# Rounding feed-forward weights to eight bits: absolute value on ScalarE, maximum on VectorE, additions on GpSimd, blocks in pairs

## The reference

```python
def _l2_normalize_complex(z):
    return z / jnp.sqrt(jnp.sum(jnp.abs(z) ** 2, axis=-1, keepdims=True))
def _quantized_matmul(x, w, scale):
    wq = w.astype(jnp.float8_e4m3fn).astype(x.dtype)
    return jnp.einsum('bsi,io->bso', x, wq) * scale

# x: (4, 512, 512) f32; W_q, W_kv, W_o: (512, 512); gate_w, up_w: (512, 1536); down_w: (1536, 512)
n = layernorm(x)
q, kv = (n @ W_q.T), (n @ W_kv.T)            # as (4, 512, 16 heads, 32)
qf  = _l2_normalize_complex(jnp.fft.fft(q, axis=-1))
kvf = jnp.cumsum(_l2_normalize_complex(jnp.fft.fft(kv, axis=-1)), axis=1)
x = x + jnp.fft.ifft(qf * kvf, axis=-1).real.reshape(4, 512, 512) @ W_o.T
n = layernorm(x)
fuse = silu(_quantized_matmul(n, gate_w, gate_scale)) * _quantized_matmul(n, up_w, up_scale)
out = x + _quantized_matmul(fuse, down_w, down_scale)
```

## Time and profile before

| | |
|---|---|
| median of three runs | 485.88 us |
| the profiled execution: time, span | 485.9 us, 483.9 us |
| TensorE busy | 439.1 us (91%) |
| VectorE busy | 315.1 us (65%) |
| ScalarE busy | 169.1 us (35%) |
| GpSimd busy | 174.2 us (36%) |
| loads and stores | 26.14 MB, mean 54 GB/s |

### The profile page before, as it was taken

One profiled execution on the slowest core, in us unless ns is written; L12 is line 12 of the kernel. 1 busy time (PEld: TensorE's weight loads), 2 busy tenths in 40 slices (PEclk: granted clock), 3 DMA queues, 4 the chain that ended last, 5 costly groups with the idle time before them and its releaser, 6 DMA issues.

```text
span 483.9 us, 5568 instructions
## 1 busy us (share of the span) xinstructions
PE 439.1 (91%) x1976; PEld 283.8 (59%) x1976; DVE 315.1 (65%) x542; ACT 169.1 (35%) x280; POOL 174.2 (36%) x161
## 2 busy tenths in 40 slices
PE   5997888997667979999998999999999999999995
PEld 4783465674333636667754666677655676555554
DVE  5999797999999966733585456443685536432234
ACT  3724433433321314533352335224533334222230
POOL 0485565686565875103006541040044400300002
PEclk9997998999898979999999999999999999999999
DMA  8933021323112300006000010013000000110002
GB/s 249 365 90 128 0 67 43 89 87 108 45 44 88 88 23 22 1 1 218 0 2 0 9 36 0 1 63 113 1 0 2 0 1 0 44 45 1 0 0 87
DMA packets 14811, 26.14 MB, mean 54 GB/s; under 512 B 2112, under 2 KB 2368, under 8 KB 14784
## 3 DMA queue, kind: packets, MB, share of 16 engines
q1 hardware_dynamic: 14496, 25.77, 16.5%
q10 hardware_dynamic: 288, 0.02, 0.0%
HBM read 21.57 MB, written 4.19 MB: 53 GB/s over the span
## 4 chain that ended last, share of the span: by engine, by line
PE 59%; DVE 6%; POOL 3%; issue 2%; ACT 1%; DVEq 0%; POOLq 0%
PE bg L383 14%; PE bd L399 14%; PE bu L383 14%; PE ba L307 9%; PE ba L341 6%; DVE qk L780 2%; PE ba L320 1%; PE ba L350 1%; POOL qk L1056 1%; POOL qk L1045 1%; POOL ks L1047 1%; DVE mq L705 1%; DVE hT L716 1%; PE ba L329 1%; DVE tu L797 1%
## 5 line engine op out<-in xcount | busy, mean ns | idle before, releaser
L399 PE MATMUL bd<-dw,fu 128*128 128x512 f32 x376 | 99.9, 408 | 3.9 <-DVE fu L852 3.9
L383 PE MATMUL bu<-hT,gu 128*128 128x512 f16 x384 | 93.0, 386 | 7.4 <-DVE ff L847 7.4
L383 PE MATMUL bg<-hT,gu 128*128 128x512 f16 x384 | 92.8, 385 | 0.5 <-ACT sl L569 0.5
L399 PEld LDWEIGHTS bd<-dw,fu 128*128 128x128 f32 x376 | 70.0, 190 | 20.0 <-DVE fu L852 4.9
L847 DVE SCALAR_TENSOR_TENSOR ff<-bu,us,sl 128x512 f32<-128x512 f32 x48 | 35.9, 748 | 66.1 <-PE bu L383 64.3
L383 PEld LDWEIGHTS bu<-hT,gu 128*128 128x128 f16 x384 | 38.0, 100 | 55.2 <-DVE ff L847 8.9
L307 PE MATMUL ba<-wf,xTs 128*128 128x512 f32 x288 | 69.1, 395 | 1.1 <-DVE wf L696 1.1
L1065 POOL TENSOR_TENSOR h<-ff,h 128x512 f32<-128x512 f32 x14 | 17.5, 1281 | 128.3 <-DVE ff L869 128.3
L383 PEld LDWEIGHTS bg<-hT,gu 128*128 128x128 f16 x384 | 35.3, 99 | 47.8 <-issue 11.3
L307 PEld LDWEIGHTS ba<-wf,xTs 128*128 128x128 f32 x288 | 54.0, 188 | 13.2 <-DVE wf L696 1.3
L569 ACT ACTIVATE sl<-bg,gs 128x512 f32<-128x512 f32 x48 | 33.0, 687 | 64.3 <-PE bg L383 63.5
(11 more groups left out here) (159 smaller groups left out, 529.8 us busy)
## 6 DMA issues: line engine op xcount, KB each, us to landing
h<-x_dram SPq DMA_DIRECT2D x16, 256.0 KB, 4.0
out_dram<-h SPq DMA_DIRECT2D x16, 256.0 KB, 2.0
hT<-gate_w_dram SPq DMA_DIRECT2D x12, 256.0 KB, 2.7
xTr<-xT_dram SPq DMA_DIRECT2D x12, 256.0 KB, 3.3
hT<-up_w_dram SPq DMA_DIRECT2D x12, 256.0 KB, 2.6
hT<-down_w_dram SPq DMA_DIRECT2D x12, 256.0 KB, 2.6
hT<-w_q_dram SPq DMA_DIRECT2D x4, 256.0 KB, 4.0
gu<-w_kv_dram SPq DMA_DIRECT2D x4, 256.0 KB, 5.7
```

Source lines behind the costliest of these rows:

```text
L383: m = e.matmul(bk[:, :], gu[:, c, 4 * w + k, col:col + P], hT[:, b % 2, part, k, :], start=k == 0 and part == 0, stop=k == KT - 1 and part ...
L399: m = e.matmul(bd[t][:, :], fu_at(n)[:, part, P * t:P * t + P], dw[:, i, :], start=i == 0 and part == 0, stop=i == NI - 1 and part == 1)
```

## The change

- The blocks are taken in pairs: 18 pairs of 128x1024, each loaded by one DMA, each step one instruction over the pair.
- `m` is now found in two steps. ScalarE takes the absolute value times 2^20, rounded to bf16 (`act_size`), and VectorE takes the maximum with a constant, in place (`dve_unit`). For gate and up `m` lies in the place of the rounded weights, for down in `mq`.
- The additions are on GpSimd for 16 pairs (`pool_round`) and on VectorE for pairs 10 and 11 (`dve_round`).
- The first eight pairs go around four pair places, that is eight blocks: the old four and the four of `h` for batch 1, which hold xT of batch 0 before and x of batch 1 after. Later pairs use the two old pair places.
- `ROUNDING`, its table of steps and the places go. Steps are written out ahead of the loop; in it, `SIZES` and `ROUNDS` say for each iteration of batch 0 which pairs are done at its end. SyncE issues the loads of all pairs ahead of the other loads and stores of the loop.
- `E` and `Q` are used again for results of the head norms in place of `ya` and `yy`.

ScalarE has `act_size` 0 and 1 behind the copies of the folds of q and of k, 2 behind the first two projections, 3 behind the next two, 4 behind the first two `act_ks`, 5 behind the last two, 6 ahead of the third `act_pT`, 7 behind the first projection pair of batch 1. In the loop it stands at the end of the iteration, ahead of `act_x`.

```diff
+NPR = 18
+NEAR = 8
+SIZES = {0: (8, 9), 1: (9, 11), 2: (11, 12), 3: (12, 13), 4: (13, 14), 5: (14, 15), 6: (15, 16), 7: (16, 17), 8: (17, 18)}
+ROUNDS = {0: (7, 9), 1: (9, 10), 3: (12, 13), 4: (13, 14), 5: (14, 15), 6: (15, 16), 7: (16, 17), 8: (17, 18)}
 def tenancies():
...
-        mq = sb("mq", [P, 3, 512], BF16)
+        mq = sb("mq", [P, 2, 2, 512], BF16)
...
+        pairs = []
         for c in range(3):
             for w, src in ((0, gate_w), (1, up_w)):
-                for k in range(KT):
-                    chunks.append((src[P * k:P * k + P, 512 * c:512 * c + 512], gu[:, c, 4 * w + k, :], c, None))
-            for i in range(4 * c, 4 * c + 4):
-                chunks.append((down_w[P * i:P * i + P, :], dw[:, i, :], c, i))
-        NC_ = len(chunks)
-        steps, rounded_on = rounding_table(NC_)
+                for k in (0, 2):
+                    pairs.append((src[P * k:P * k + 2 * P, 512 * c:512 * c + 512],
+                                  gu[:, c, 4 * w + k:4 * w + k + 2, :]))
+            for i in (4 * c, 4 * c + 2):
+                pairs.append((down_w[P * i:P * i + 2 * P, :], dw[:, i:i + 2, :]))
+        assert len(pairs) == NPR
         AT, BEFORE, LEAVES = tenancies()
+        def stage_at(n):
+            slot = 2 * (n % 4 if n < NEAR else n % 2)
+            return stage[:, slot:slot + 2, :] if slot < 4 else h[:, 1, slot - 4:slot - 2, :]
+        def stage_before(n):
+            if n < NEAR:
+                return (n - 4 if n > 3 else None), n // 4 + 1
+            return (n - 4 if n < NEAR + 2 else n - 2), (NEAR // 4 + (n - NEAR) // 2 + 1)
+        def size_at(n):
+            return mq[:, n % 2, :, :] if n % 6 > 3 else pairs[n][1].bitcast(BF16)
         def rounded(n):
-            what, count = rounded_on[n]
-            return (p_rd if what == "p" else v_rd), count
-        def rounded_all(ns):
-            on = {}
-            for n in ns:
-                what, count = rounded_on[n]
-                on[what] = max(on.get(what, 0), count)
-            return [(p_rd if what == "p" else v_rd, count) for what, count in on.items()]
+            if n in (10, 11):
+                return v_rd, n - 9
+            return p_rd, (n + 1 if n < 10 else n - 1)
+        def stage_landed(n):
+            return d_st[n % 4 if n < NEAR else n % 2], 16 * stage_before(n)[1]
...
+        def act_size(e, n):
+            e.wait_ge(*stage_landed(n))
+            if n == 6:
+                e.wait_ge(s_fold, 8)
+            if n == 12:
+                e.wait_ge(s_wohi, KT)
+            if n % 6 > 3 and n > 5:
+                e.wait_ge(*rounded(n - 6))
+            e.activation(size_at(n), stage_at(n), ACT.Abs, scale=2.0 ** 20).then_inc(a_size, 1)
...
-        def dve_expo(e, n):
-            m = mq[:, n % 3, :]
-            top = stage[:, n % 4, :].bitcast(U16).rearrange("p (n t) -> p n t", t=2)[:, :, 1]
-            e.wait_ge(d_st[n % 4], 16 * (n // 4 + 1))
-            if n >= 3:
-                e.wait_ge(*rounded(n - 3))
-            e.tensor_scalar(m.bitcast(U16), top, 0x7F80, 0x0040, ALU.bitwise_and, ALU.bitwise_or).then_inc(v_ex, 1)
-            e.wait_ge(v_ex, 2 * n + 1)
-            e.tensor_scalar(m, m, 1.5 * 2.0 ** -6, 2.0 ** 20, ALU.max, ALU.mult).then_inc(v_ex, 1)
-        def round_chunk(e, n):
-            what, count = rounded_on[n]
-            _, dst, c, i = chunks[n]
-            added, done = (p_add, p_rd) if what == "p" else (v_add, v_rd)
-            piece, m = stage[:, n % 4, :], mq[:, n % 3, :]
-            e.wait_ge(v_ex, 2 * n + 2)
-            e.tensor_tensor(piece, piece, m, ALU.add).then_inc(added, 1)
-            e.wait_ge(added, count)
-            if i is None and c == 2 and n % 12 == 0:
-                e.wait_ge(s_wohi, KT)
-            if i is None and c == 1 and n % 12 == 0:
-                e.wait_ge(s_fold, 8)
-            e.tensor_tensor(dst, piece, m, ALU.subtract).then_inc(done, 1)
-        def dve_spare(e, place):
-            for what, n in steps.get(place, ()):
-                if what == "e":
-                    dve_expo(e, n)
-                elif what == "d":
-                    round_chunk(e, n)
+        def dve_unit(e, n):
+            e.wait_ge(a_size, n + 1)
+            e.tensor_scalar(size_at(n), size_at(n), 1.5 * 2.0 ** 14, None, ALU.max).then_inc(v_unit, 1)
+        def dve_round(e, n):
+            e.wait_ge(v_unit, n + 1)
+            e.tensor_tensor(stage_at(n), stage_at(n), size_at(n), ALU.add).then_inc(v_add, 1)
+            e.wait_ge(v_add, rounded(n)[1])
+            e.tensor_tensor(pairs[n][1], stage_at(n), size_at(n), ALU.subtract).then_inc(v_rd, 1)
...
+                    if b == 0 and i in SIZES:
+                        for pair in range(*SIZES[i]):
+                            dve_unit(e, pair)
+                        if i in (2, 3):
+                            dve_round(e, 8 + i)
...
+        def pool_round(e, first, end):
+            for n in range(first, end):
+                e.wait_ge(v_unit, n + 1)
+                e.tensor_tensor(stage_at(n), stage_at(n), size_at(n), ALU.add).then_inc(p_add, 1)
+                e.wait_ge(p_add, rounded(n)[1])
+                e.tensor_tensor(pairs[n][1], stage_at(n), size_at(n), ALU.subtract).then_inc(p_rd, 1)
...
         def gpsimd_program(e):
             pool_x(e, 0, 0)
             pool_x(e, 0, 1)
-            for place in ("a0", "a1", "a2", "a3", "a4"):
-                pool_spare(e, place)
+            pool_round(e, 0, 4)
             pool_ks(e, 0, 0)
             pool_ks(e, 0, 1)
-            pool_spare(e, "a5")
+            pool_round(e, 4, 5)
             pool_product(e, 0, 0)
-            pool_spare(e, "p0")
             pool_ks(e, 0, 2)
             pool_ks(e, 0, 3)
             pool_product(e, 0, 1)
+            pool_round(e, 5, 6)
             pool_product(e, 0, 2)
-            pool_spare(e, "p1")
             pool_product(e, 0, 3)
-            pool_spare(e, "p2")
-            pool_spare(e, "p3")
-            pool_x(e, 1, 0)
-            pool_x(e, 1, 1)
-            pool_spare(e, "p4")
-            pool_x(e, 1, 2)
-            pool_x(e, 1, 3)
-            for place in ("p5", "p6", "p7", "p8", "p9", "p10", "p11", "p12"):
-                pool_spare(e, place)
+            for k in range(KT):
+                pool_x(e, 1, k)
+            pool_round(e, 6, 7)
...
                         if i == 4:
                             pool_product(e, nxt, 0)
-                    if b == 0:
-                        pool_spare(e, f"split{i}")
-                        if i == 1:
-                            pool_spare(e, "stats")
-                    if nxt < NB and 5 <= i <= 7:
-                        pool_product(e, nxt, i - 4)
-                    if b == 0:
-                        pool_spare(e, f"end{i}")
+                        if 5 <= i <= 7:
+                            pool_product(e, nxt, i - 4)
+                    if b == 0 and i in ROUNDS:
+                        pool_round(e, *ROUNDS[i])
...
+        def sp_weights(e, first, end):
+            for n in range(first, end):
+                before, _ = stage_before(n)
+                if before is not None:
+                    e.wait_ge(*rounded(before))
+                elif n >= 2:
+                    for k in (2 * n - 4, 2 * n - 3):
+                        e.wait_ge(a_x, k + 1)
+                        e.wait_ge(*x_low_done(0, k))
+                e.dma_start(stage_at(n), pairs[n][0].rearrange("(k p) n -> p k n", p=P)).then_inc(stage_landed(n)[0], 16)
...
-            for place in ("a0", "a1", "a2", "a3", "a4", "a5", "p0"):
-                sp_spare(e, place)
-            sp_x(e, 1)
-            for place in ("p1", "p2", "p3", "p4"):
-                sp_spare(e, place)
+            sp_weights(e, 4, 8)
             sp_xT(e, 1, 2)
             sp_xT(e, 1, 3)
-            for place in ("p5", "p6", "p7", "p8", "p9", "p10", "p11", "p12"):
-                sp_spare(e, place)
+            sp_weights(e, 8, 10)
+            sp_x(e, 1)
+            sp_weights(e, 10, NPR)
```

More of the change, by code:

```diff
@@ L45, in constants @@
             np.concatenate([inv, tri, ones], 1).astype(np.float32))
-ROUNDING = {
[5 rows of a table removed]
[L54 to L70, removed]
-            if what == "e":
[L72 to L80, removed]
+NPR = 18
+NEAR = 8
+SIZES = {0: (8, 9), 1: (9, 11), 2: (11, 12), 3: (12, 13), 4: (13, 14), 5: (14, 15), 6: (15, 16), 7: (16, 17), 8: (17, 18)}
+ROUNDS = {0: (7, 9), 1: (9, 10), 3: (12, 13), 4: (13, 14), 5: (14, 15), 6: (15, 16), 7: (16, 17), 8: (17, 18)}
 def tenancies():
@@ L145, in build @@
         S = sb("S", [P, NT, 32], F32)
-        E, Q, y0, ya, yy = (sb(n, [P, NT, 33], F32) for n in ("E", "Q", "y0", "ya", "yy"))
+        E, Q, y0 = (sb(n, [P, NT, 33], F32) for n in ("E", "Q", "y0"))
         rv = sb("rv", [P, NT], F32)
@@ L174, in build @@
         a_pT, a_hT, a_silu, a_fu, a_wohi, a_wolo = (sem("act_" + n) for n in ("pT", "hT", "silu", "fu", "wohi", "wolo"))
```

(48 more changed lines are left out.)

76 lines of the change are left out of this document (18 added, 58 removed), and 5 rows, old and new, of the table ROUNDING.

## The result

The changed kernel took 493.8 us (median of 4 runs, 492.55 to 494.63) against 485.85 us (4 runs, 484.51 to 486.64): ratio 1.0164, 95% interval 1.013 to 1.0199. It is 8.0 us slower. Its profiled execution took 494.63 us, with a span of 492.6 against 483.9 before: 8.7 us to explain.

The account below looks back on a forecast made before the run. The prediction took VectorE, with the rounding on it, to bound two stages. Its terms, 3.8 + 0.9 + 0 + 6.1 - 0.3 (iteration 8) = +10.5 us on 485.9, gave 496.4 us, own range 491 to 501, whole range 484 to 503.

Parts of the forecast that it names:

- Iteration 7: Batch 0's loop: xT of batch 2, queued behind pair 17's weights, holds ScalarE and GpSimd; +6.1 us (+2 to +7.5).
- Rival A: The late xT is hidden, so iteration 7 ends as before: 490.3 us; chance 0.17.
- The chain of 12.8 us a tile: Iterations 3 to 6: rounding on GpSimd stands in series behind the product, 7.9 + 4.3 + 0.6 us a tile.
- Rival B: GpSimd's rounding of pairs 13 to 15 falls into its waits, 12.9 us come back: 483.5 us; chance 0.14.
- Iterations 3 to 6: Batch 0's loop: freed exponents are eaten by rounding on VectorE and in GpSimd's chain; 0 us (-4 to +2).
- Before the loop: GpSimd's longer additions delay VectorE's norms and the products ahead of batch 0's loop; +3.8 us (-2 to +6).
- (a): Before the loop: pairs 0 to 3 back to back on GpSimd make the first scaling start at 39.7, +0.5 us.
- (b): Before the loop: pair 4 ahead of the first product on GpSimd runs over the second norm head, +2.1 us.
- (c): Before the loop: pair 5 between products 1 and 2 on GpSimd starts product 2 at 62.9, +4.8 us.
- Iteration 0: Batch 0's loop: the seventh absolute value stands ahead of the first silu on ScalarE; +0.9 us (0 to 1.1).
- Rival C: Longer locks cost more: six more scalings and splits up to 173 us wait a microsecond each: 502 us; chance 0.12.
- Rival D: The absolute value needs its own activation table, 18 loads, over half on the path: about 507 us; chance 0.02.

Follow-up runs that it names:

- Experiment 1: The changed kernel with the two xT loads of batch 2 issued ahead of the last weights in SyncE's order: 488.52 us, ratio 1.0065.
- Experiment 2: Experiment 1's kernel with GpSimd's additions of pairs 13, 14 and 15 over 16 instead of 512 columns: 474.9 us, ratio 0.9782.
- experiment 6: Experiment 1's kernel, pairs 9 to 12 an iteration earlier on GpSimd, VectorE rounding nothing, pairs 14 to 16 between sum and product: 477.48 us, ratio 0.9822.
- experiment 4: The changed kernel with pairs 4 and 5 on GpSimd behind product 3 and the xT subtractions, not ahead of products 0 and 2: 493.65 us, ratio 1.0169.
- experiment 8: Experiment 6's kernel, seventh absolute value behind the first silu, pairs 4 to 6 written into GpSimd's iteration 0, pair 9 into iteration 1: 477.83 us, ratio 0.9836.
- experiment 9: The changed kernel with pairs 4 to 6 on GpSimd behind a wait for the last norm (gated): 484.12 us against 484.1, ratio 1.0003.
- experiment 7: Experiment 6's kernel with pairs 4 and 5 placed as in experiment 4 and the seventh absolute value behind the first silu: 476.99 us, ratio 0.9814.
- experiment 3: The changed kernel with each GpSimd addition split into two instructions of 512 elements: 493.94 us, ratio 1.017.
- experiment 5: Experiment 4's kernel with GpSimd's additions in instructions of 512 elements: 491.01 us, ratio 1.0111.
- replan4: Experiment 8's kernel with experiment 9's wait ahead of pair 4: 470.8 us, ratio 0.9714.

## Why the prediction was right, and where its terms were off

**What bounds the kernel.** VectorE did bound two stages by its busy time. With 46 us less on it in all, product 0 left GpSimd 6.1 us sooner after the start of iteration 3 (+22.3 for +28.4); pair 13 ahead of the carry took most of that back, and 2.2 us were left at the sum of tile 2. The work moved to GpSimd came back as waits.

**Iteration 7 (+6.1, measured +5.9): right in place and price.** ScalarE's 10.66 us wait for xTr and GpSimd's 5.09 behind it are the two rows that I had named. The sum of tile 3 came 18.75 us after tile 2's (19.3 predicted), iteration 8 19.7 after it (19.9). Experiment 1 took the cause away and got 5.3 us back. Rival A falls.

**The chain of 12.8 us a tile: right.** Measured 12.83. Experiment 2 took 11.3 us of three pairs out of the chain and got all of it, and 2.3 us more by the medians. Rival B needed sums less than about 10 us apart; experiment 6 made them so (9.9 for tiles 1 to 2, 11.0 for 2 to 3) by moving the pairs, and there the kernel is faster by 1.8%, with pairs 10 and 11 off VectorE too. The rival described a real mechanism, for another order of the same instructions.

**Iterations 3 to 6 (0, measured -2.2): mis-sized, and most of what the forecast was too high by.** I had product 0 leave GpSimd at +23.5 and pair 13 wait for its maximum until +25.4. They came at +22.3 (141.49) and +23.25 (142.45), so the carry started at +27.6, not +29.9: 1.2 us from the product, 1.0 from the maximum. The instructions themselves are as taken: 2.14 for an addition, 0.41 for a maximum.

**Before the loop (+3.8, measured +4.6): the sum was close, its parts less so.** VectorE in the changed kernel:

```profile
38.70 1.29 DVE L764 TENSOR_TENSOR qk<-qk,sc 128x512 f32<-128x512 f32 x2 [0.27 <-DVE sc L756]
...
46.11 2.06 DVE L731 TENSOR_SCALAR E<-mv 128x2 f32<-128x2 f32 x1
...
73.37 1.27 DVE L747 SCALAR_TENSOR_TENSOR E<-E 128x2 f32<-128x2 f32 x1
...
79.80 1.13 DVE L807 TENSOR_SCALAR E<-mv 128x2 f32<-128x2 f32 x1
```

(a) The first scaling came 0.5 us earlier than before, not later; that the exponents taken out outweighed the longer waits is my reading, not tested. (b) A norm instruction of two elements did wait 2.06 us for one of GpSimd's, and norm head 2 ends 1.0 us late (48.92 for 47.96), not 2.1. (c) Product 2 starts 3.45 late (61.58 for 58.13), not 4.8: the 4.3 us of pair 5 are as taken, but GpSimd came to them only 0.8 us late, not 2.1.

What I had put at nothing ahead of the loop is TensorE's clock. The output projection of tile 1, before and after:

```profile
62.33 2.99 PE L341 MATMUL bd<-wo,fu 128*128 128x512 f32 x12 [1.46 <-DVE fu L806]
```

```profile
65.61 4.58 PE L325 MATMUL bd<-wo,fu 128*128 128x512 f32 x12 [1.46 <-DVE fu L790]
```

It starts 3.3 us late and takes 1.6 longer, at a granted clock of 0.61 (65.6 to 70.0) where it was 1.00. The projection of tile 2 is then 4.0 late (70.38 for 66.36), that of tile 3 as well, the last transposes 4.6 (82.69 for 78.09), the loop 4.6. So pair 6, which I took at the price of the two blocks that it replaced, costs about 0.6 us against the kernel before, although the last norm waits for GpSimd (73.37, 79.80): in the kernel before, the norm met GpSimd's work too (two scalings of 1.00 us took 2.88 at 69.47). Experiments 4 and 8 move this cost about, and experiment 9 removes it. How much of the 10.2 us each of pairs 4, 5 and 6 holds by itself was not measured; a version almost without the additions of pairs 4 and 5, meant for that, gave no time.

**Iteration 0 (+0.9, measured +0.8): right.** TensorE waited 0.66 us for the first silu; with the absolute value behind it, iteration 0 is 0.8 us shorter (experiment 7).

**Rival C (longer locks, 502): not for the time of the kernel as it is** (experiment 3, no change, with 1.9 us gained before the loop and 1.6 lost in it), but 3.6 us at the start of the loop where GpSimd works without a gap (experiments 4 and 5), and the main part of the wait in iteration 4 of the kernels of experiments 6 and 10 (2.02 and 2.98 us; read from the traces, not tested). The Trainium skill, "SBUF — State Buffer", section "Who interferes with whom", says that the holder of the port pair keeps it for its whole instruction; 0.16 us growing to 2.04 and, with halves, to 1.07 agrees.

**Rival D falls:** the absolute values took 1.04 to 1.12 us, and the trace has 14 table loads, as before.

In all, three costs stand against the relief of VectorE: about 5 us for the queue (experiment 1), 4.3 us for each pair in the chain (2), and 8 to 10 us for rounding pairs 4 to 6 ahead of the loop (9), where the kernel before paid something too (its loop starts 5.6 us after the gated one's). replan4 takes all three away, but not in full.

## What to carry to other kernels

Relieving the busiest engine buys nothing when the moved work stands in series in the chain of another: put it into the receiving engine's waits, between its last result and the operand it waits for, where two tiles' chains were 5.5 us shorter (experiment 6). Work written further down in an engine's program starts no later unless something ahead of it waits (experiments 4 and 8): where work must keep out of a stretch, gate it. SyncE issues loads in program order, so a load behind one that waits for a buffer is as late as that buffer (xT at 172.51, behind the pair that waited until 172.02): issue loads in the order of first use.

## What the runs showed of the hardware

- An addition or subtraction of 32-bit tensors in SBUF on GpSimd (in the rounding with `m` in bf16 as the second) takes 0.73 us for 256, 1.16 for 512 and 2.14 for 1024 elements a partition, and 0.25 for 2 x 16.
- VectorE instructions of two elements, 0.16 us alone, took up to 2.06 us beside GpSimd's additions of 2.14, and one got in after each of them.
- A stall can cost TensorE more than its length: behind 0.98 us of idle time twelve f32 products took 2.99 us, behind 2.46 us 4.28; eight f16 products took 3.46 us behind the 9.64 us wait, at a granted clock of 0.53 (182.4 to 185.8), and 1.90 at 1.00, about the ratio of 1.2 to 2.4 GHz. The wait just ahead does not tell it alone: behind 1.46 us twelve f32 products took 2.99 us in the kernel before and 4.58 in the changed one, where the clock had also been at 0.52 from 53.6 to 59.5.
